# The last head group of a top-32 attention split between ScalarE and VectorE, and a masked product in halves of two PSUM banks

## The reference, cut to what matters

```
scores = jnp.einsum('bhsd,bhtd->bhst', q, k) / scale      # 8 x 16 heads, D = 8
top_s, top_i = jax.lax.top_k(scores, 32)
probs = jax.nn.softmax(top_s, axis=-1)
out = jnp.einsum('bhsk,bhskd->bhsd', probs, v_g)          # v_g: the chosen values
return out.transpose(0, 2, 1, 3).reshape(b, s, e) @ Wo.T + bo
```

## Time and profile before

| | |
|---|---|
| median of 3 runs | 2515.19 us (2509.85, 2515.19, 2515.55) |
| the profiled execution | 2510.24 us, span 2508.4 us |
| busy share: PE, DVE, ACT, POOL | 75%, 69%, 45%, 28% |
| granted TensorE clock, mean | 0.81 |
| `delta_outputs`: first mask to end of the last | 705.03 to 749.90 us |
| `topk_attention`: first score to the last add to the stream | 1524.78 to 2295.91 us |

### The profile page before, as it was taken

How to read it: one execution, slowest core, us unless ns; L and a number is a source line. 1 busy time by engine, 2 the same in 40 slices (tenths; PEclk the granted TensorE clock), 3 DMA queues, 4 the chain that set the end, 5 groups by cost and what they waited for, 6 DMA issues and landing times. The chain is left out here.

```text
span 2508.4 us, 36866 instructions
## 1 busy us (share of the span) xinstructions
PE 1871.5 (75%) x11751; PEld 1113.4 (44%) x11763; DVE 1736.4 (69%) x5543; ACT 1134.2 (45%) x3143; POOL 711.7 (28%) x620
## 2 busy tenths in 40 slices
PE   6996889853877999979997875565555555555778
PEld 2654447442445666644464553343333333333443
DVE  4236342267765666657746777999999999995655
ACT  3653442251315777731233654555555555454411
POOL 1200045014432333310032411444433433332130
PEclk8997899965998999989998896666666566566979
DMA  5000001400000000000200000000000000000000
GB/s 212 2 1 1 27 27 29 151 14 1 2 2 1 2 2 1 0 1 0 94 2 1 1 1 1 1 1 1 1 1 1 1 1 1 1 1 1 1 1 17
DMA packets 10591, 37.76 MB, mean 15 GB/s; under 512 B 1344, under 2 KB 7488, under 8 KB 9136
## 3 DMA queue, kind: packets, MB, share of 16 engines
q1 hardware_dynamic: 8880, 33.04, 3.4%
q0 software_dynamic: 1536, 2.59, 0.4%
HBM read 30.15 MB, written 5.51 MB: 14 GB/s over the span
## 5 line engine op out<-in xcount | busy, mean ns | idle before, releaser
L3719 PE MATMUL psum<-work 32*128 32x256 f32 x512 | 130.5, 654 | 291.8 <-ACT work L3829 291.8
L3888 DVE MATCH_REPLACE8 work<-work 128x256 f32<-128x256 f32 x768 | 304.8, 405 | 0.0
L3936 POOL TENSOR_TENSOR work<-work 128x1024 f32<-128x1024 f32 x64 | 150.6, 2354 | 494.5 <-ACT work L3829 494.5
L3885 DVE MAX8 work<-work 128x8 f32<-128x256 f32 x768 | 266.1, 406 | 0.0
L3719 PEld LDWEIGHTS psum<-work 32*128 32x128 f32 x512 | 77.6, 311 | 318.2 <-ACT work L3829 161.8
L709 POOL TENSOR_TENSOR work<-work 128x256 f32<-128x256 f32 (+2 forms) x144 | 133.3, 944 | 225.9 <-DVE work L997 225.9
L925 ACT ACTIVATE work<-work 128x128 f32<-128x128 f32 (+1 forms) x320 | 144.9, 454 | 19.1 <-DVE work L972 17.3
L3829 ACT ACTIVATE work<-work 128x256 f32<-128x256 f32 x256 | 128.4, 502 | 0.0
L3742 PE MATMUL psum<-work,tiles 128*8 128x256 f32 x512 | 117.2, 610 | 13.6 <-ACT work L3838 13.6
L3938 POOL TENSOR_TENSOR work<-work 128x1024 f32<-128x1024 f32 x64 | 121.1, 1892 | 6.2 <-DVE work L3910 1.2
L3827 ACT ACTIVATE work<-psum,work 128x256 f32<-128x256 f32 x256 | 117.4, 459 | 0.0
(11 more groups left out here) (616 smaller groups left out, 4629.3 us busy)
## 6 DMA issues: line engine op xcount, KB each, us to landing
big_weights<-L0f_dram SPq DMA_DIRECT2D x1, 6117.5 KB, 29.3
big_weights<-L_dram SPq DMA_DIRECT2D x1, 5772.0 KB, 17.5
big_weights<-L_dram SPq DMA_DIRECT2D x1, 4952.5 KB, 15.8
choice_rows<-tiles SPq DMA_DIRECT2D x2, 1024.0 KB, 10.5
tiles<-choice_rows SPq DMA_DIRECT2D x8, 256.0 KB, 5.0
big_weights<-L_dram SPq DMA_DIRECT2D x1, 2027.0 KB, 20.2
big_weights<-L_dram SPq DMA_DIRECT2D x1, 1630.5 KB, 13.8
big_weights<-L0f_dram SPq DMA_DIRECT2D x1, 1630.5 KB, 6.4
```

The source lines that it names most:

```text
L3719: mm = nc.tensor.matmul(scores(n)[:, u, :], qb[head, tile % 2, u % 2 * P:(u % 2 + 1) * P], kb[head, tile % 2, :], start=True, stop=True, t ...
L3885: ch.step(v.max(top8[:, n % 2, u, r, :], src[:, u, :]))
L3888: ins = v.match_replace(raw[:, n % 2, u, :], top8[:, n % 2, u, r, :], src[:, u, :], REPLACED)
L3936: ch.link(g.tensor_tensor(mine, mine, rest[:, n % 2], ALU.subtract))
```

## The change

In `delta_outputs` scores, masks and their signals go in two halves: heads 0 and 1 (banks 0 and 1), then heads 2 and 3 (banks 2 and 3). `score(n)` waits for and signals each half by itself; the mask is two instructions of 128x768; `mix` waits for both.

In `topk_attention` only the last group (`FINAL`, number 63) is treated otherwise. ScalarE copies the turned group 62 before it softens group 63, not after it. `soften` signals each of the four blocks; VectorE, not GpSimd, subtracts and scales each block (128x256) as it comes; `turn` signals its two heads apart, ScalarE copies the first (one bank) and VectorE the second (`turned_copied_s`); three of the four matmuls of the last `put_out` go ahead of the last turn, the fourth behind the last mix; and VectorE adds the product with its bias to the stream in one instruction, in place of ScalarE and GpSimd.

```diff
@@ -2664,20 +2664,21 @@
...
                 b, e = units[n]
                 src = (q_even, q_odd)[e]
-                if n >= 1:
-                    pe.wait_ge(c.scores_masked.sem, c.scores_masked.at(n))
-                for j in range(4):
-                    nc.tensor.matmul(scores(j)[:, 0:3:2, :], k[band[j], b * S:b * S + P], src[band[j], b * S:(b + 1) * S],
-                                     start=True, stop=True, tile_position=(32 * j, 0))
-                for j in range(4):
-                    mm = nc.tensor.matmul(scores(j)[:, 1, :], k[band[j], b * S + P:(b + 1) * S],
-                                          src[band[j], b * S + P:(b + 1) * S], start=True, stop=True,
-                                          tile_position=(32 * j, 0))
-                mm.then_inc(c.scores_ready.sem, 1)
+                for half in range(2):
+                    if n >= 1:
+                        pe.wait_ge(c.scores_masked.sem, c.scores_masked.at(2 * n - 1 + half))
+                    for j in (2 * half, 2 * half + 1):
+                        nc.tensor.matmul(scores(j)[:, 0:3:2, :], k[band[j], b * S:b * S + P], src[band[j], b * S:(b + 1) * S],
+                                         start=True, stop=True, tile_position=(32 * j, 0))
+                    for j in (2 * half, 2 * half + 1):
+                        mm = nc.tensor.matmul(scores(j)[:, 1, :], k[band[j], b * S + P:(b + 1) * S],
+                                              src[band[j], b * S + P:(b + 1) * S], start=True, stop=True,
+                                              tile_position=(32 * j, 0))
+                    mm.then_inc(c.scores_ready.sem, 1)
 
             def mix(n):
                 b, e = units[n]
-                pe.wait_ge(c.scores_masked.sem, c.scores_masked.at(n + 1))
+                pe.wait_ge(c.scores_masked.sem, c.scores_masked.at(2 * n + 2))
                 if n == 0:
@@ -2743,12 +2744,14 @@
...
                 if n < len(units):
                     b, e = units[n]
-                    dve.wait_ge(c.scores_ready.sem, c.scores_ready.at(n + 1))
                     if n >= 2:
                         dve.wait_ge(c.mixed_ready.sem, c.mixed_ready.at(n - 1))
-                    v.tensor_tensor(probs[n % 2], c.psum[:, 0:4, 0:3 * P].rearrange("p j (a x) -> p j a x", x=P),
-                                    masks[:, b % 4].unsqueeze(1).broadcast_to([P, 4, 3, P]), ALU.mult) \
-                        .then_inc(c.scores_masked.sem, 1)
+                    for half in range(2):
+                        two = slice(2 * half, 2 * half + 2)
+                        dve.wait_ge(c.scores_ready.sem, c.scores_ready.at(2 * n + half + 1))
+                        v.tensor_tensor(probs[n % 2][:, two], c.psum[:, two, 0:3 * P].rearrange("p j (a x) -> p j a x", x=P),
+                                        masks[:, b % 4].unsqueeze(1).broadcast_to([P, 2, 3, P]), ALU.mult) \
+                            .then_inc(c.scores_masked.sem, 1)
                 if n % 2 == 1 and 3 <= n < len(units) + 3:
@@ -3656,6 +3660,7 @@
...
     SCALE = float(D ** -0.5)
     NG, GROUPS, TILES = H // 2, B * H // 2, B * H // 4
+    FINAL = GROUPS - 1
     a = Arena(c)
@@ -3732,6 +3737,8 @@
...
                 b, tile = n // NG, n // 2
                 pe.wait_ge(c.turned_copied.sem, c.turned_copied.at(n + 1))
+                if n == FINAL:
+                    pe.wait_ge(c.turned_copied_s.sem, c.turned_copied_s.at(1))
                 if n == 0:
@@ -3744,13 +3751,14 @@
...
                 mm.then_inc(c.mixed_ready.sem, 1)
 
-            def put_out(b):
-                pe.wait_ge(c.out_copied.sem, c.out_copied.at(4 * b + 4))
+            def put_out(b, lo, hi):
+                pe.wait_ge(c.out_copied.sem, c.out_copied.at(4 * b + hi))
                 pe.wait_ge(c.qk_taken.sem, c.qk_taken.at(min(4 * b + 7, TILES)))
-                for j in range(4):
+                for j in range(lo, hi):
                     mm = nc.tensor.matmul(bank(7)[:, 0:S], wo[:, j, :], attended[:, b % 2, j, :], start=(j == 0),
                                           stop=(j == 3))
-                mm.then_inc(c.out_product.sem, 1)
+                if hi == 4:
+                    mm.then_inc(c.out_product.sem, 1)
 
@@ -3764,6 +3772,9 @@
...
                             mm = nc.tensor.transpose(bank(4 + head)[:, at:at + P],
                                                      probs[:, n % 2, 2 * head + q, kt * P:(kt + 1) * P], ident)
+                    if n == FINAL and head == 0:
+                        mm.then_inc(c.probs_turned.sem, 1)
+                        pe.wait_ge(c.probs_picked.sem, c.probs_picked.at(n + 2))
                 mm.then_inc(c.probs_turned.sem, 1)
@@ -3794,7 +3805,9 @@
...
                     mix(t - 2)
                 if t >= 10 and (t - 10) % NG == 0:
-                    put_out((t - 10) // NG)
+                    put_out((t - 10) // NG, 3 if t == GROUPS + 2 else 0, 4)
+                if t == GROUPS:
+                    put_out(B - 1, 0, 3)
                 if piece_at(t) is not None:
@@ -3828,13 +3841,14 @@
...
                     ins = nc.scalar.activation(rest[:, s, u, :], raw[:, s, u, :], ACT.Exp, bias=nbias[:, s, u:u + 1],
                                                scale=SCALE)
-                ins.then_inc(c.probs_ready.sem, 1)
+                    if n == FINAL or u == U - 1:
+                        ins.then_inc(c.probs_ready.sem, 1)
 
...
                 if n >= 2:
                     act.wait_ge(c.mixed_ready.sem, c.mixed_ready.at(n - 1))
-                for head in range(2):
+                for head in range(1 if n == FINAL else 2):
                     ins = nc.scalar.copy(turned[:, n % 2, head].rearrange("p t s -> p (t s)"), bank(4 + head))
@@ -3859,15 +3873,17 @@
...
             take_queries(0)
             for t in range(GROUPS + 4):
+                if t == GROUPS:
+                    take_turned(t - 2)
                 if 0 <= t - 1 < GROUPS:
                     soften(t - 1)
-                if 0 <= t - 2 < GROUPS:
+                if 0 <= t - 2 < GROUPS and t != GROUPS:
                     take_turned(t - 2)
...
                 if t % 2 == 1 and 0 <= t - 3 < GROUPS:
                     take_heads((t - 3) // 2)
-                if t >= 10 and (t - 10) % NG == 0:
+                if t >= 10 and (t - 10) % NG == 0 and t < GROUPS + 2:
                     take_output((t - 10) // NG)
@@ -3920,10 +3936,25 @@
...
                     dve.wait_ge(c.scores_max.sem, c.scores_max.at(n + 1))
                     ch.clear()
-            last = GROUPS - 1
+            s = FINAL % 2
             dve.wait_ge(c.kept_summed.sem, c.kept_summed.at(GROUPS))
-            dve.wait_ge(c.probs_picked.sem, c.probs_picked.at(GROUPS - 2))
-            v.reciprocal(rsum[:, last % 2, :], sums[:, last % 2, :]).then_inc(c.sums_inverted.sem, 1)
+            dve.wait_ge(c.probs_picked.sem, c.probs_picked.at(FINAL))
+            v.reciprocal(rsum[:, s, :], sums[:, s, :]).then_inc(c.sums_inverted.sem, 1)
+            for u in range(U):
+                mine = probs[:, s, u, :]
+                dve.wait_ge(c.probs_ready.sem, c.probs_ready.at(GROUPS + u))
+                ch.link(v.tensor_tensor(mine, mine, rest[:, s, u, :], ALU.subtract))
+                if u == 0:
+                    dve.wait_ge(c.sums_inverted.sem, c.sums_inverted.at(GROUPS))
+                ins = v.tensor_scalar(mine, mine, rsum[:, s, u:u + 1], None, ALU.mult)
+                if u % 2:
+                    ins.then_inc(c.probs_picked.sem, 1)
+            dve.wait_ge(c.probs_turned.sem, c.probs_turned.at(GROUPS + 1))
+            v.tensor_copy(turned[:, s, 1].rearrange("p t s -> p (t s)"), bank(5)).then_inc(c.turned_copied_s.sem, 1)
+            dve.wait_ge(c.out_product.sem, c.out_product.at(B))
+            seq = sequence(B - 1)
+            v.scalar_tensor_tensor(c.X[:, seq], bank(7)[:, 0:S], c.w("L3a_bo"), c.X[:, seq], ALU.add, ALU.add)
+            ch.clear()
 
@@ -3953,8 +3984,8 @@
...
                     ch.link(g.tensor_tensor(x, x, c.w("L3x_vmask").unsqueeze(1).broadcast_to([P, CH // P, P]), ALU.mult))
 
-            for t in range(GROUPS + 4):
-                if 0 <= t - 1 < GROUPS:
+            for t in range(GROUPS + 3):
+                if 0 <= t - 1 < FINAL:
                     pick(t - 1)
...
```

More of the change, by code:

```diff
@@ L2771, in _ @@
             ch.clear()
-    for s, n in ((c.updates_moved, 4), (c.updates_placed, 4), (c.scores_ready, len(units)), (c.scores_masked, len(units)),
+    for s, n in ((c.updates_moved, 4), (c.updates_placed, 4), (c.scores_ready, 2 * len(units)),
+                 (c.scores_masked, 2 * len(units)),
                  (c.mixed_ready, len(units)), (c.out_copied, B), (c.out_turned, B), (c.heads_scaled, B), (c.gated, B),
@@ L3965, in topk_attention @@
                  (c.turned_copied, GROUPS), (c.mixed_ready, GROUPS), (c.out_copied, TILES), (c.out_product, B),
```

(5 more changed lines are left out.)

## The result

| | before | changed |
|---|---|---|
| median of all runs, 19 each | 2512.14 us (2508.24 to 2517.43) | 2503.69 us (2493.70 to 2513.05; one execution of 2916.77, at a mean clock of 0.60, is left out of the ratio) |
| ratio, 95% interval | | 0.9962 [0.9951, 0.9973] |
| profiled execution | 2510.24 us, span 2508.4 | 2493.70 us, span 2491.9 |
| `delta_outputs`: first mask to the end of the last | 44.87 us | 39.71 us |
| `topk_attention`: last choice to the last add to the stream | 19.28 us | 10.21 us |

The kernel is faster by 0.38%, 9.5 us by the ratio and 8.5 by the medians. The profiled execution is 16.5 us faster, the fastest of the 19: the two blocks and what lies behind the second give 5.2 + 9.1 + 1.2 = 15.5 of it. That is one execution: the 19 together give 9.5 [6.8, 12.3], less than the 15.5 of the three stretches, and no trace shows where the rest goes.

A forecast was written before the change was run, and what follows sets the result against it. VectorE and TensorE taking turns on four banks bound `delta_outputs`, a chain of one engine at a time the tail of `topk_attention`; -4.6 - 7.1 = -11.7 us, giving 2498.5 or 2503.5 by level, forecast 2502 us, range 2495.5 to 2510.

The forecast's parts named there:

- Half a mask: In `delta_outputs`, a 128x768 mask on VectorE was put at 0.95 us, against 1.76 for a whole one.
- The bound of 1.22: In `delta_outputs`, upper limit for a half mask in us, at which the block would change by +0.2 us.
- the rival of 1.76: In `delta_outputs`, a half mask costs as much as a whole, 1.76 us; total +6.5, 2521 us; chance 0.03.
- Half a score is a whole one on TensorE: In `delta_outputs`, two row bands need as long as four: same 0.87 us until a mix, 1.00 until the mask.
- The rival of bands in order: In `delta_outputs`, second half score waits until the first's passes are issued: 5.15 us a pair, total -10.4, 2504; chance 0.08.
- The drained rival: In `delta_outputs`, a wait between halves drains the first: 5.6 to 5.8 us a pair, total -6 to -8, 2508; chance 0.13.
- The loop: In `delta_outputs`, the VectorE and TensorE cycle for a pair of units takes 4.99 us against 5.63 before.
- The block: `delta_outputs` as a whole gains 4.6 us, with bounds of -9.3 and +0.2.
- The tail: In `topk_attention`, from last choice to last add: 12.2 us against 19.3, a gain of 7.1.
- the bound of 1.7: In the tail of `topk_attention`, 1.7 us more gained if TensorE's clock rises early; not in the sum.
- The norm behind it: Block after `topk_attention`: up to +3 us allowed if it starts at TensorE's lower clock.
- the clock rival: Tail gains 7.1 us but the next norm block runs at the lower clock, +3; total -8.7, 2506.5; chance 0.13.

The follow-up runs named there:

- e5: Kernel before with each mask written as two of 128x768, scores left whole; masks 9 to 15 took 17.27 us against 16.89 before.
- e9: Changed kernel with the second half of each score waiting for the first half's products; a pair 5.81 us, masks 9 to 15 17.42 us.
- e1: Kernel before with only the halves in `delta_outputs` changed; ratio to before 0.9983 [0.9972, 0.9994], median 2512.42 us.
- e7: Changed kernel with all four output matmuls of the last sequence behind the last mix; last choice to last add 14.59 us.
- e3: The changed kernel timed again, beside its two parts; ratio to before 0.9953 [0.9935, 0.9972], median 2501.26 us.
- e2: Kernel before with only the last group of `topk_attention` changed; ratio to before 0.9962 [0.9947, 0.9978], median 2506.43 us.
- e8: Changed kernel with unit 0's scores ahead of the placements and the second placement in bank 6; ratio to before 0.9954, median 2501.82 us.
- e11: Changed kernel with unit 0's scores ahead of the placements and the tail's last copy split between ScalarE and VectorE; ratio to before 0.9968, tail 9.94 us.

## Why the prediction was right, point by point

- **Half a mask** was put at 0.95 us: the two rows of halves give 1.82 for two with an overlap, single ones 0.94 to 0.96. The bound of 1.22 and the rival of 1.76 are gone: all 32 half masks take 0.944 to 0.958 us, as they do in e5 (0.946 to 0.958), where TensorE writes no scores beside them.
- **Half a score is a whole one on TensorE**, and the second may start beside the first: right (e9, and the rows around 709.5). The rival of bands in order falls with it: it needed 5.15 us a pair. The Trainium skill (TensorE: Matmul & The Clock Gate, Part 3, The mechanism) has matmuls start strictly in program order; here a matmul of another band started 0.19 us ahead of one written before it (709.88 and 710.07), so for separate row bands the measurement goes against the rule and decides. The drained rival is what e9 makes: 5.81 us a pair, where 5.6 to 5.8 had been said.
- **The loop** of 4.99 us a pair was 4.93, step by step the one forecast (1.83 + 0.05 + 0.87 + 0.87 + 0.37 + 1.00 against 1.82 + 0.06 + 0.85 + 0.79 + 0.37 + 1.04); the placements, said to lose their cover at 0.8 us each, cost 0.87 (the pairs from mask 2 to 4 and from 4 to 6 take 5.80 us each in the changed trace, not 4.93).
- **The block**: -4.6 forecast, -5.2 in the traces, of which 0.7 is the second score: it ran at the lower clock before and not in the changed trace. -4.3 by e1's ratio.
- **The tail**: -7.1 forecast, -9.1 measured. This is the term that was mis-sized, by 2.0 us: the clock's rise stood beside the sum, as a bound, and not in it. Counted from the last choice: the softening starts at +0.44 (0.47 forecast); VectorE's fourth block ends at +5.90 (6.19), since a pair keeps up with ScalarE's 0.755 us; then TensorE at 2.4 GHz makes it +7.49 for the last mix (8.14), +8.99 for the output (10.5), +10.21 for the add (12.2). The 12.2 less the bound of 1.7 and the 0.3 of VectorE's blocks are the 10.2 measured. The rise came in all seven executions profiled with the whole tail, and in e7 it did not come before the add.
- **The norm behind it**: up to +3 allowed, -1.2 measured with all that follows. The norm itself was 1.4 us longer (16.5 against 15.1), the blocks behind it 2.5 shorter. So the clock rival was right inside the norm, by half of its 3 us, and wrong for the total; that the blocks behind would get more back was not foreseen.
- **The sum**: -11.7 forecast, -9.5 [-12.3, -6.8] in the first 19 runs, -11.8 in e3, -13.9 as the sum of e1 and e2, -15.5 as the stretches of the traces. The 2502 us of the forecast, between two levels of before, met 2503.69. That the figure came so near is in part luck: the stretches gained 3.8 us more than forecast and the whole gained 2.2 less, and single executions of the changed kernel spread over 19 us.

## What to carry to other kernels

Half of an instruction need not be half the price: VectorE's mask went from 1.76 us to 0.95, TensorE's row-packed score only from 0.75 to 0.70, and the gain came from letting the two engines work on different banks at once. Where one engine is nearly full afterwards, count again what had lain in its slack: the two placements took back 1.7 us. In a tail of one engine after the other, moving work forward paid twice here, since TensorE's clock rose behind the early matmuls and not without them (e7), and edits of one such chain can't be priced one by one: the three here were worth 15.7 us taken out singly and 9.1 together.

## What the runs showed that was not expected

- The tail takes 10.20 to 10.22 us in seven executions, clock rise and all, while the same unchanged code ahead of it varies: `delta_outputs` starts anywhere from 698.5 to 711.8 us, and from its last instruction to the first score of `topk_attention` it is 766.9 to 778.5 us. Single times can't weigh edits of a few us, then, and a block's own rows can. Not all of this is chance from one execution to the next: in e5 to e8, four kernels on one chip, the second stretch agrees within 0.5 us.
- A matmul of one row band of TensorE can start before one of another band that is written ahead of it (709.88 and 710.07).
- Moving one score ahead of the placements gave 1.6 us in its block and timed 4 to 8 us better twice on one chip, but no better than the change in e8 and e11, which hold the same move; shortening the tail by 0.27 us came with 4.2 us more behind it.
